# Three PSUM banks in a fixed order, a projection two chunks late and re-dealt weight splits in a fused linear-attention layer

## The chip, the cores and the metric

The kernel runs on one NeuronCore of a Trainium2 chip. The metric is the device time of one execution in microseconds (us); three executions of the kernel before took 1916.09, 1921.84 and 1921.94 us (median 1921.84).

## What is computed

x has 2048 rows (tokens) of 512 values. The layer is a gated linear attention with a small expert mixture ahead of it and behind it:

```python
x = x + 0.5 * ffn(layernorm(x))        # router of 64, top 8, mix of expert biases
x = x + attn(layernorm(x))
x = x + 0.5 * ffn(layernorm(x))

# attn: 32 query heads, 8 key/value heads, D = 128, chunks of 128 tokens
q, k, v = rope(x @ Wq.T), rope(x @ Wk.T), x @ Wv.T
dt = softplus(x @ Win.T + dt_bias);  g = dt * A;  G = cumsum(g) within a chunk
y_intra = (q @ k.T * decay) @ (v * dt)             # inside a chunk, causal
y_inter = (q * exp(G)) @ state                     # from the chunks before
state   = state * exp(G_last) + (k * exp(G_last - G)).T @ (v * dt)
y = (y_intra + y_inter) / rms * gnorm_w * silu(x @ Wg.T)
out = y @ Wo.T
```

## The kernel before

Every float32 operand of a large product is split into two bfloat16 halves, hi (a rounded copy) and lo (what is left), and each product is three matmuls, hi by hi, lo by hi and hi by lo (`mm3`, L288 to L290). So wherever a matrix is made, ScalarE (ACT) writes the hi half and VectorE (DVE) or GpSimd (POOL) subtracts for the lo half.

**The order of the work.** After a first mixture stage, the attention runs over 8 key/value heads g (called groups here), each with its 4 query heads. A group has 16 steps n, one for each chunk of 128 tokens, and s = n mod 4 is the step's place in a block of four. Each engine has a written-out order of its operations in its own `step` function, and semaphores alone tie the engines together; an engine never passes an operation that waits. Beside the attention of chunk n, the steps also compute the projections of the next block of 512 tokens, ten "fills" per block: item 0 is the key, items 1 to 4 the four query heads, item 5 the value and items 6 to 9 the gates of four chunks. `FILLS` says which item stands in slot A, B or C of which step.

On TensorE a step is: scores of chunk n+1, slot A, `read_state` (the state's part of the output), `turn_z` (transposes of the gated output z of chunk n-1), `attend` (the part inside the chunk, and the state update), slots B and C, in s=1 the key transposes, and `project_out` (z of chunk n-1 by Wo).

**PSUM.** The fills and the output projections share two banks in turn (`RING`, L150), numbered by `ring_order`. A writer waits until the use before the last of the ring is free (L692, L778). The fills of items 0 to 4 are read by ACT (`swap`, L867: two half copies into QS) and by DVE (`rotate`, L1220: product with cos into QF, L1233, which frees the bank; later the sum with the sine part, L1237, after POOL's `times_sin`, L1078). The value is read by ACT and DVE (`values`, `v_lo`), a gate by ACT (tanh into TH, L894) and DVE (`silu2`, L1253), and the output of a projection by DVE (`add_out`, L1333, into ACC). One further bank, B_T, takes the transposes of z and of the keys.

**The output of a chunk.** DVE multiplies the state's part by exp(G) (`combine`, L1276), adds it to the inner part (L1280); ACT squares it with a running sum (`square`, L936), POOL makes the inverse root (`inv_rms`, L1117 and L1120), DVE multiplies it with the gate (`gated`, L1313); after the transpose ACT and DVE split it (`zt_hi`, L943, `zt_lo`, L1329). The decay of the scores goes over POOL's `mask_rows` (L1091), ACT's `decay` (L907), DVE's `decayed` (L1267), ACT's `p_hi` (L913) and POOL's `p_lo` (L1113); the weighted value over POOL's `weighted_v` (L1101), ACT's `wv_hi` (L920) and POOL's `wv_lo` (L1109); the state over DVE's `update_state`, ACT's `state_hi` and DVE's `state_lo`.

**The weights.** A group needs 14 pieces of 128x512: 0 to 9 for the fills (four of them the gate's) and 10 to 13 for Wo. They are loaded into two staging buffers in turn (`STAGE`, `load_piece`, L325), so load i waits for the lo half of piece i-2. ACT writes the hi half (`split_hi`, L854; Wo is multiplied by half the norm's gain on the way), DVE or POOL the lo half (`w_lo` L1322, `wo_lo` L1317, `split_lo` L1070). Pieces 0 to 9 of the next group are split in steps 10 to 13 (`EARLY` on DVE, `MID` on POOL), the four Wo pieces all in step n=1 of the group itself, on ACT and DVE. The fills of the next group begin in step 12, and the projection with the new Wo in n=1.

**The loop.** Step 0 of the first group is written ahead, groups 0 to 6 are a loop of steps 1 to 16, and the last group is written out. A piece of code that ends the kernel is the second mixture stage.

Of the kernel before, what the change touches and what calls it, by code (L numbers as in the profile page):

```python
# [22 lines left out]
P = 128  # L23
# [3 lines left out]
G = H // KVH  # L27
# [15 lines left out]
FILLS = {0: {"A": 0, "B": 1, "C": 2}, 1: {"A": 3, "B": 4, "C": 5}, 2: {"A": 6, "B": 7}, 3: {"A": 8, "C": 9}}  # L43

EARLY = {10: (0, 1), 11: (3, 4), 12: (6,), 13: (8,)}
MID = {10: (2,), 11: (5,), 12: (7,), 13: (9,)}
LOADS = {1: (0, 1), 10: (2, 3, 4), 11: (5, 6, 7), 12: (8, 9), 13: (10, 11)}
N_EARLY = sum(len(i) for i in EARLY.values())
FIRST = len(FILLS[0])


def steps(last):

    return range(1, NCH if last else NCH + 1)
# [7 lines left out]
def ring_order(last):  # L62

    seq = []
    for n in steps(last):
        f = filled(n, last)
        seq += [("F", n // BLK, f[x]) for x in "ABC" if x in f] + [("W", n - 1)]
    if last:
        seq.append(("W", NCH - 1))
    order = {u: r for r, u in enumerate(seq)}  # L70
    order[("W", -1)] = -1
    return order


def turn_order(last):

    seq = []
    for n in steps(last):
        seq.append(("Z", n - 1))
        if n % BLK == 1 and filled(n, last):  # L80
            seq.append(("K", n // BLK))
    if last:
        seq.append(("Z", NCH - 1))
    return {u: r for r, u in enumerate(seq)}
# [12 lines left out]
def build(nc, x, cos, sin, masks, wall, rwt, rb, eb2, wint, dtb, alog, gn, out):  # L97
    rows_dram = nc.dram_tensor("rows_dram", (NCH, KVH, GW), F32).ap()
    with ExitStack() as ctx:
# [31 lines left out]
        NGT = sb("NGT", [P, NB, P])  # L131
# [18 lines left out]
        RING = BANK[0:2]  # L150
# [7 lines left out]
        with ExitStack() as over:  # L158
            MASKS, ONES, DTB, ALOG, SPD, GF = memory(over, (
                ("MASKS", [P, 3, P], F32), ("ONES", [P, P], F32), ("DTB", [P, H], F32), ("ALOG", [P, H], F32),  # L160
                ("SPD", [P, 2, 7, BLK * H], F32), ("GF", [P, NCH * H], F32)))
# [8 lines left out]
        SQ = sb("SQ", [P, G, P])  # L170
# [3 lines left out]
        ZTH = sb("ZTH", [P, GW], BF16)  # L174
        ZTL = sb("ZTL", [P, GW], BF16)
# [18 lines left out]
        QF = sb("QF", [P, 2, TB])  # L194
# [11 lines left out]
        TH = sb("TH", [P, GW])  # L206
# [1268 lines left out]
```

## Time and profile before

| | |
|---|---|
| three runs | 1916.09, 1921.84, 1921.94 us |
| the profiled execution | 1920.05 us, span 1918.3 us |
| mean granted TensorE clock | 0.967 |
| TensorE (PE) busy | 1712.5 us, 89% |
| weight loads (PEld) | 980.7 us, 51% |
| DVE | 1483.4 us, 77% |
| ACT | 1114.1 us, 58% |
| POOL | 1172.3 us, 61% |

All numbers come from one execution of the program, taken by the hardware profiler. Lines are those of the kernel's source. In a row of the timeline the first number is the start in us from the span's start, the second the duration; a bracket gives the engine's idle time before and the operation that ended it. Matmuls are pipelined: the next starts before the record of the one before ends. The clock column is the granted TensorE clock as a share of 2.4 GHz.

### The profile page before, as it was taken

How to read it: one execution, taken by the hardware profiler on the slowest of the kernel's cores; microseconds unless marked ns; L12 is line 12 of the kernel's file. 1: busy time of each engine (PE TensorE's matmuls, PEld its weight loads, DVE VectorE, ACT ScalarE, POOL GpSimd, SP SyncE). 2: the span in 40 equal slices, each digit the busy share in tenths (PEclk: the TensorE clock that was granted, in tenths of full speed). 3: DMA queues.
4: the chain of work that ended last, by engine and by line, in shares of the span. 5: the costliest groups of instructions: out<-in, count | busy, mean ns of one | idle time of the engine just before them, and what ended most of it. 6: DMA issues, size and time to landing. Idle time of an engine off the chain costs nothing.

```text
span 1918.3 us, 39511 instructions
## 1 busy us (share of the span) xinstructions
PE 1712.5 (89%) x11652; PEld 980.7 (51%) x11652; DVE 1483.4 (77%) x3212; ACT 1114.1 (58%) x3012; POOL 1172.3 (61%) x1084
## 2 busy tenths in 40 slices
PE   5657998989988998989988998999988998999976
PEld 5534554555545554555545554555545554555544
DVE  6976778787787778777787778778887778787875
ACT  5445556656665656656665565655665655665643
POOL 1236667656666667657665666656765766666643
PEclk8779999999999999999999999999999999999997
DMA  4110101110111001110111002110111002110002
GB/s 165 34 32 30 33 23 56 40 44 20 40 56 41 23 23 62 34 46 18 40 55 41 23 23 63 33 46 23 43 48 46 18 23 67 28 34 23 23 1 88
DMA packets 38532, 77.20 MB, mean 40 GB/s; under 512 B 4769, under 2 KB 5793, under 8 KB 37153
## 3 DMA queue, kind: packets, MB, share of 16 engines
q1 hardware_dynamic: 38304, 74.47, 12.6%
q8 instruction: 107, 1.75, 0.4%
q14 instruction: 121, 0.98, 0.2%
HBM read 69.99 MB, written 4.46 MB: 39 GB/s over the span
## 4 chain that ended last, share of the span: by engine, by line
PE 46%; issue 18%; DVE 15%; ACT 12%; POOL 7%; DVEq 1%; ACTq 1%; DMA 0%; POOLq 0%
PE B L288 14%; PE B L290 13%; PE B L289 13%; ACT SQ L936 3%; ACT QS L873 2%; DVE QF L1237 2%; PE B L774 2%; POOL ROWS L1091 2%; DVE QF L1233 1%; ACT QS L872 1%; PE B L455 1%; DVE PF L1267 1%; DVE YF L1276 1%; DVE ZTL L1329 1%; POOL WVF L1101 1%
## 5 line engine op out<-in xcount | busy, mean ns | idle before, releaser
L1113 POOL TENSOR_TENSOR PL<-PF,PH 128x512 bf16<-128x512 f32 x128 | 155.7, 1217 | 393.4 <-ACT PH L913 393.4
L288 PE MATMUL B<-WH,XTH 128*128 128x512 bf16 (+1 forms) x1024 | 295.2, 308 | 67.0 <-DVE QF L1233 57.0
L289 PE MATMUL B<-WL,XTH 128*128 128x512 bf16 (+1 forms) x1024 | 294.5, 307 | 0.0
L290 PE MATMUL B<-WH,XTL 128*128 128x512 bf16 (+1 forms) x1024 | 294.2, 307 | 0.0
L1078 POOL TENSOR_TENSOR QS<-QS,SIN 128x512 f32<-128x512 f32 x160 | 215.4, 1346 | 71.5 <-ACT QS L873 71.5
L288 PE MATMUL B<-XTH,WH 128*128 128x512 bf16 x640 | 242.7, 379 | 15.0 <-DVE G L1253 10.9
L290 PE MATMUL B<-XTH,WL 128*128 128x512 bf16 x640 | 242.6, 379 | 0.0
L289 PE MATMUL B<-XTL,WH 128*128 128x512 bf16 x640 | 242.6, 379 | 0.0
L288 PE MATMUL B<-WH,ZTH 128*128 128x512 bf16 x512 | 194.5, 380 | 36.9 <-DVE QF L1233 22.7
L913 ACT ACTIVATE PH<-PF 128x512 bf16<-128x512 f32 x128 | 80.7, 631 | 238.2 <-DVE PF L1267 238.1
L1329 DVE TENSOR_TENSOR ZTL<-B,ZTH 128x512 bf16<-128x512 f32 x128 | 88.1, 688 | 149.7 <-ACT ZTH L943 149.7
L290 PE MATMUL B<-WH,ZTL 128*128 128x512 bf16 x512 | 194.0, 379 | 0.0
L289 PE MATMUL B<-WL,ZTH 128*128 128x512 bf16 x512 | 194.0, 379 | 0.0
L1091 POOL TENSOR_TENSOR ROWS<-ROWS,AFTER 128x512 f32<-128x512 f32 x128 | 191.0, 1492 | 0.0
L936 ACT ACTIVATE SQ<-B 128x128 f32<-128x128 f32 x512 | 134.1, 276 | 84.8 <-DVE B L1280 83.4
L288 PEld LDWEIGHTS B<-WH,XTH 128*128 128x128 bf16 x1024 | 104.6, 102 | 149.5 <-DVE QF L1233 59.0
L907 ACT ACTIVATE PF<-ROWS,NG 128x128 f32<-128x128 f32 x512 | 162.6, 396 | 13.7 <-issue 13.7
L1267 DVE SCALAR_TENSOR_TENSOR PF<-B,DT,PF 128x128 f32<-128x128 f32 x512 | 143.8, 344 | 34.0 <-ACT PF L907 32.6
L920 ACT ACTIVATE WVH<-WVF 128x512 bf16<-128x512 f32 x120 | 75.6, 630 | 160.3 <-POOL WVF L1101 158.4
L1109 POOL TENSOR_TENSOR WVL<-WVF,WVH 128x512 bf16<-128x512 f32 x120 | 139.8, 1165 | 45.4 <-ACT WVH L920 45.4
L1313 DVE SCALAR_TENSOR_TENSOR YF<-B,RR,G 128x128 f32<-128x128 f32 x512 | 143.2, 341 | 7.3 <-POOL RR L1120 7.3
L1120 POOL TENSOR_TENSOR RR<-RM,HALF 128x4 f32<-128x4 f32 x128 | 137.1, 1071 | 19.0 <-POOL RM L1117 17.7
(160 smaller groups left out, 4539.9 us busy)
## 6 DMA issues: line engine op xcount, KB each, us to landing
ROWS<-rows_dram SPq DMA_DIRECT2D x128, 256.0 KB, 3.1
STAGE<-in_wall SPq DMA_DIRECT2D x112, 256.0 KB, 2.6
ACC<-in_x SPq DMA_DIRECT2D x4, 1024.0 KB, 7.6
out<-ACC SPq DMA_DIRECT2D x3, 1024.0 KB, 3.9
COS<-in_cos SPq DMA_DIRECT2D x1, 1024.0 KB, 12.6
SIN<-in_sin SPq DMA_DIRECT2D x1, 1024.0 KB, 14.4
out<-ACC SPq DMA_DIRECT2D x4, 256.0 KB, 2.5
EBF<-in_eb SPq DMA_DIRECT2D x1, 256.0 KB, 4.3
```

The costliest lines, as they stand in the source:

```text
L288: nc.tensor.matmul(out_, ah, bh, start=first, stop=False)
L289: nc.tensor.matmul(out_, ah, bl, start=False, stop=False)
L290: return nc.tensor.matmul(out_, al, bh, start=False, stop=last)
L907: ins = nc.scalar.activation(PF[:, c], ROWS[:, n % 2, c], ACT.Exp, bias=tab(NG, g, n)[:, h:h + 1], scale=-1.0)
L936: ins = nc.scalar.activation(SQ[:, h, :], B_PV[:, h * P:(h + 1) * P], ACT.Square, scale=float(P) ** -0.5, accum_out=SS[:, h:h + 1])
L1078: nc.gpsimd.tensor_tensor(QS[:, sl, :], QS[:, sl, :], SIN[:, t0:t0 + TB], ALU.mult).then_inc(sin_ready.sem, 1)
L1091: nc.gpsimd.tensor_tensor(rows, rows, AFTER[:, None, :].broadcast_to([P, G, P]), ALU.add).then_inc(rows_masked.sem, 1)
L1109: nc.gpsimd.tensor_tensor(WVL[:, :], WVF[:, :, :].rearrange("p h e -> p (h e)"), WVH[:, :], ALU.subtract).then_inc(wvl_ready.sem, 1)
L1113: nc.gpsimd.tensor_tensor(PL[:, n % 2, :], PF[:, :], PH[:, n % 2, :], ALU.subtract).then_inc(pl_ready.sem, 1)
L1120: nc.gpsimd.tensor_tensor(RR[:, :], RM[:, :], HALF[:, :], ALU.pow).then_inc(rr_ready.sem, 1)
L1267: ins = nc.vector.scalar_tensor_tensor(PF[:, c], B_S[:, c], dt[:, h:h + 1], PF[:, c], ALU.mult, ALU.mult)
L1313: ins = nc.vector.scalar_tensor_tensor(YF[:, c], B_PV[:, c], RR[:, h:h + 1], G2[:, s + b % 2 * (s == BLK - 1), c], ALU.mult, ALU.mult)
```

## The change

1. **Banks.** The ring has three banks (0, 1, 3). Which fill and which projection uses which one is written down (`FILL_BANK`, `OUT_BANK`, and `OUT_BANK_END` for the last steps), and so is whose release a writer waits for (`AFTER_FILL`, or the `add_out` of chunk n-3). Fills and outputs have semaphores of their own.
2. **Projection.** `project_out` in step n is that of chunk n-2; in s=1 it stands ahead of slot B, otherwise at the end. ZTH and ZTL have two buffers. The key transposes move from s=1 to s=2, `keys_lo` to s=3.
3. **Gain.** The norm's gain is applied when z is split (`zt_hi`, `zt_lo`), no longer to Wo.
4. **Splits.** All 14 pieces go by the same code. `HI`, `LO_POOL`, `LO_DVE` and `LOADS` deal them over steps 9 to 13 and, for Wo, steps 17 and 18 (n = 1 and 2 of the next group). ACT copies at the end of its step (in s=1 ahead of slot C, in s=2 ahead of the keys), POOL subtracts after wv_lo, DVE after `gated` and ahead of slot B.
5. **Scaling.** ACT multiplies the state's part by exp(G), four 128x128 pieces into YF (`scale_inter`), between `zt_hi` and `wv_hi`; DVE's product is gone.
6. **Orders.** ACT computes the decay of chunk n+2 late in step n rather than that of n+1 at its start; POOL masks rows after `weighted_v`; item 4's lo half moves from DVE to the end of POOL's step s=2; QF has four buffers; item 9 moves to slot B.
7. **Memory.** The squares go into YF, the tanh into its slot of G2, NGT shares memory with the set-up tensors.
8. **The loop** covers steps 3 to 18; steps 0 to 2 are written ahead (`PEEL`).

```diff
+PEEL = 3
+FILLS = {0: {"A": 0, "B": 1, "C": 2}, 1: {"A": 3, "B": 4, "C": 5}, 2: {"A": 6, "B": 7}, 3: {"A": 8, "B": 9}}
+FILL_BANK = (0, 1, 2, 1, 0, 1, 2, 0, 2, 1)
+OUT_BANK = (0, 2, 1, 2)
+OUT_BANK_END = {10: 1, 11: 2, 12: 0, 13: 1, 14: 0, 15: 1}
+AFTER_FILL = {0: 3, 1: 2, 3: 2, 5: 2, 7: 3, 8: 2}
...
-EARLY = {10: (0, 1), 11: (3, 4), 12: (6,), 13: (8,)}
-MID = {10: (2,), 11: (5,), 12: (7,), 13: (9,)}
-LOADS = {1: (0, 1), 10: (2, 3, 4), 11: (5, 6, 7), 12: (8, 9), 13: (10, 11)}
+HI = {9: (0,), 10: (1, 2), 11: (3, 4, 5), 12: (6, 7, 8), 13: (9,), 17: (10, 11), 18: (12, 13)}
+LO_POOL = {9: (0,), 10: (1,), 11: (3, 5), 12: (6, 7), 13: (9,), 17: (10,), 18: (12,)}
+LO_DVE = {10: (2,), 11: (4,), 12: (8,), 17: (11,), 18: (13,)}
+LOADS = {3: (0, 1), 9: (2,), 10: (3, 4), 11: (5, 6, 7), 12: (8, 9), 13: (10, 11), 18: (12, 13)}
...
-        RING = BANK[0:2]
+        RING = (BANK[0], BANK[1], BANK[3])
...
+            def bank_free(g, n, item, use):
...
+                elif item in AFTER_FILL:
+                    pe.wait_ge(ring_free.sem, ring_free.at(g, use - AFTER_FILL[item]))
+                else:
+                    pe.wait_ge(out_free.sem, out_free.at(g, n - 3))
...
+            def scale_inter(g, n):
...
+                act.wait_ge(inter_full.sem, inter_full.at(g, in_event(n)))
+                eg = tab(EG, g, n)
+                for h in range(G):
+                    c = slice(h * P, (h + 1) * P)
+                    ins = nc.scalar.activation(YF[:, c], B_IN[:, c], ACT.Copy, scale=eg[:, h:h + 1])
+                ins.then_inc(inter_read.sem, 1)
...
-                nc.scalar.activation(ZTH[:, :], B_T[:, :], ACT.Copy).then_inc(zth_ready.sem, 1)
+                nc.scalar.activation(ZTH[:, n % 2, :], B_T[:, :], ACT.Copy, scale=GNH[:, 0:1]).then_inc(zth_ready.sem, 1)
...
-                nc.vector.tensor_tensor(YF[:, :].rearrange("p (h e) -> p h e", h=G), B_IN[:, :].rearrange("p (h e) -> p h e", h=G),
-                                            tab(EG, g, n)[:, :, None].broadcast_to([P, G, P]), ALU.mult).then_inc(inter_read.sem, 1)
```

The new order of a step on DVE, in full (`now` is the step's fills; TensorE, ACT and POOL have new orders of the same kind):

```python
if nxt: decayed(g, n + 1)
if s == 1 and now: add(FILLS[0]["C"])
if s == 2 and now: v_lo(g, b + 1, use(PV_)); add(FILLS[1]["B"])
if s != 2 and n >= PEEL: add_out(g, n - 3, last)
if s == 1 and now: q_lo(g, b + 1, FILLS[0]["B"])
if s == 3 and now: keys_lo(g, b + 1)
if now: slot("A")
combine(g, n); update_state(g, n)
if n: zt_lo(g, n - 1)
if s < 2 and now: add(now["A"])
state_lo(g, n)
gated(g, n)
if s == 1 and n >= PEEL: add_out(g, n - 2, last)
if s == 1 and now: q_lo(g, b + 1, FILLS[0]["C"])
for i in weights_at(LO_DVE, n, last): w_lo(g + 1 if n >= PEEL else g, i)
if now: slot("B")
if s == 0 and now: add(now["B"]); slot("C")
```

ACT: `p_hi`(n+1), hi of the item before (s=1), slot A, hi (s=2), `zt_hi`(n-1), `scale_inter`, hi (s=1), `wv_hi`(n+1), `square`, `state_hi`, slot B (s other than 1), hi of A (s=0), `decay`(n+2), slot C (s=0), slot B and hi of A (s=1), the hi halves of `HI`, slot C (s=1), `keys_hi` (s=2). POOL: `p_lo`(n+1), `weighted_v`(n+1), lo of A's item of the step before (s=1, 2), sine A, `mask_rows`(n+2), `inv_rms`, sine B (s=0), `wv_lo`(n+1), lo of item 4 (s=2), sine B (s=1), the lo halves of `LO_POOL`, sine C (s=0).

## Rows read from the trace of the kernel before

**Rows 1.** The page, busy time and share of each engine, instructions.

```profile
PE 1712.5 (89%) x11652; PEld 980.7 (51%) x11652; DVE 1483.4 (77%) x3212; ACT 1114.1 (58%) x3012; POOL 1172.3 (61%) x1084
```

**Rows 2.** The line L1289: count, duration min/median/max (ns), first and last start (us).

```profile
L1289 DVE COPY ST<-B x8: 681/681/681, 167.4 to 1669.2; 128x512 f32<-128x512 f32 x8
```

**Rows 3.** Timeline of TensorE, the first matmul of four steps: start, us, operation.

```profile
622.01 0.38 PE L288 MATMUL B<-QH,KH 128*128 128x512 bf16 x1
...
632.86 0.38 PE L288 MATMUL B<-QH,KH 128*128 128x512 bf16 x1
...
643.95 0.38 PE L288 MATMUL B<-QH,KH 128*128 128x512 bf16 x1
...
657.38 0.38 PE L288 MATMUL B<-QH,KH 128*128 128x512 bf16 x1
```

**Rows 4.** Timeline of TensorE, a V fill and the transposes behind it.

```profile
666.57 0.23 PE L288 MATMUL B<-WH,XTH 128*128 128x128 bf16 x1 [0.77 <-DVE QF L1233]
...
669.26 0.28 PE L721 MATMUL B<-IDF,KF 128*128 128x128 f32 x1
```

**Rows 5.** Waits of TensorE in one group, 596.5 to 811: us in total, times, longest.

```profile
PE B L288 <- DVE QF L1233: 10.7, 8, 4.5
PE B L288 <- DVE G L1253: 3.8, 3, 1.5
PE B L288 <- issue: 1.0, 1, 1.0
```

**Rows 6.** Timeline of TensorE, the longest wait of that group, in step n=1.

```profile
614.66 0.23 PE L288 MATMUL B<-WH,XTH 128*128 128x128 bf16 x1 [4.47 <-DVE QF L1233]
```

**Rows 7.** Two stretches: us, busy us (and instructions) per engine, PEclk, DMA share, GB/s.

```profile
616.00:618.00 2.00, 2.00 (x22) 2.00 (x21) 2.00 (x7) 1.94 (x10) 1.43 (x3) 0.50 0.02 4
...
1686.50:1689.00 2.50, 2.40 (x23) 2.40 (x24) 2.47 (x8) 1.27 (x10) 2.31 (x2) 0.51 0.29 90
```

**Rows 8.** Timeline of ACT: half a swap, then four squares, ended by the state copy.

```profile
653.01 0.59 ACT L873 ACTIVATE QS<-B 64x512 f32<-64x512 f32 x1
653.62 0.28 ACT L936 ACTIVATE SQ<-B 128x128 f32<-128x128 f32 x1
...
654.63 0.64 ACT L927 ACTIVATE STH<-ST 128x512 bf16<-128x512 f32 x1
```

**Rows 9.** Groups by line and shape: busy us, mean ns | idle us before, releaser.

```profile
L1120 POOL TENSOR_TENSOR RR<-RM,HALF 128x4 f32<-128x4 f32 x128 | 137.1, 1071 | 19.0 <-POOL RM L1117 17.7
...
L1109 POOL TENSOR_TENSOR WVL<-WVF,WVH 128x512 bf16<-128x512 f32 x120 | 139.8, 1165 | 45.4 <-ACT WVH L920 45.4
...
L1233 DVE TENSOR_TENSOR QF<-B,COS 128x512 f32<-128x512 f32 x128 | 87.5, 684 | 38.8 <-ACT QS L873 37.9
...
L1276 DVE TENSOR_TENSOR YF<-B,EG 128x512 f32<-128x512 f32 x120 | 81.7, 681 | 0.3 <-PE B L774 0.3
...
L1324 DVE TENSOR_TENSOR WL<-STAGE,WH 128x512 bf16<-128x512 f32 x42 | 58.4, 1417 | 23.1 <-ACT WH L857 23.1
...
L857 ACT ACTIVATE WH<-STAGE 128x512 bf16<-128x512 f32 x80 | 48.1, 621 | 10.2 <-DMA STAGE<-in_wall 10.2
...
L1072 POOL TENSOR_TENSOR WL<-STAGE,WH 128x512 bf16<-128x512 f32 x38 | 44.9, 1185 | 34.1 <-ACT WH L857 34.1
...
L860 ACT ACTIVATE WH<-STAGE,GNH 128x512 bf16<-128x512 f32 x32 | 21.1, 708 | 0.0
```

**Rows 10.** The load of a weight piece, L331, all 112.

```profile
DMA to landing us min/median/max: 2.3/2.6/14.3
```

**Rows 11.** Timeline of TensorE, two further waits: start of the fills, last group.

```profile
128.16 0.39 PE L288 MATMUL B<-XTH,WH 128*128 128x512 bf16 x1 [3.27 <-DVE KF L1233]
...
1686.60 0.29 PE L288 MATMUL B<-WH,XTH 128*128 128x128 bf16 x1 [3.20 <-DVE QF L1233]
```

**Rows 12.** Timeline of TensorE, transposes of z in two of the last four steps.

```profile
1826.19 0.63 PE L774 MATMUL B<-IDF,YF 128*128 128x128 f32 x4 [0.44 <-DVE YF L1313]
...
1834.25 0.63 PE L774 MATMUL B<-IDF,YF 128*128 128x128 f32 x4 [0.44 <-DVE YF L1313]
```

More of the change, by code:

```diff
@@ L75, in turn_order, with use_of, z_turn, k_turn @@
[L75 to L84, printed above, removed]
+def use_of(b, item):
+    return NFILL * b + item
+def z_turn(n, last=False):
+    return n + 1 + min((max(n - 1, 0) + BLK - 1) // BLK, NB - 1 if last else 2 * NB)
+def k_turn(b):
+    return (BLK + 1) * (b - 1) + 3 if b else 0
@@ L87, in cs_event, with fill_bank, out_bank @@
+def fill_bank(use):
+    b, item = divmod(use, NFILL)
+    return FILL_BANK[item] if b else (item + 2) % 3
+def out_bank(n, last):
+    return OUT_BANK_END[n] if last and n in OUT_BANK_END else OUT_BANK[(n + 2) % BLK]
 def cs_event(n):
@@ L353, in _ @@
             load_rows(0, 2)
-            load_rows(0, 3)
             def step(g, n, last):
@@ new lines, in step, with slot @@
+                now = filled(n, last)
+                back = filled(n - 1, last) if n else {}
+                nxt = not (last and n == NCH - 1)
+                def slot(x):
+                    item = now[x]
+                    if item < PV_:
+                        swap(g, b + 1, item, use_of(b + 1, item))
+                    elif item == PV_:
+                        values(g, b + 1, use_of(b + 1, item))
+                    else:
+                        gate(g, b + 1, item - PG, use_of(b + 1, item))
@@ new lines, in step, with use, slot, add @@
+                now = filled(n, last)
+                nxt = not (last and n == NCH - 1)
+                def use(item):
+                    return use_of(b + 1, item)
+                def slot(x):
+                    if now[x] < PV_:
+                        times_cos(g, b + 1, now[x], use(now[x]))
+                    else:
+                        silu2(g, b + 1, now[x] - PG, use(now[x]))
+                def add(item):
+                    add_sin(g, b + 1, item, use(item))
+                if nxt:
+                    decayed(g, n + 1)
@@ new lines, in step @@
+                if s == 1 and now:
+                    add(FILLS[0]["C"])
+                if s == 2 and now:
+                    v_lo(g, b + 1, use(PV_))
+                    add(FILLS[1]["B"])
+                if s != 2 and n >= PEEL:
+                    add_out(g, n - 3, last)
+                if s == 1 and now:
+                    q_lo(g, b + 1, FILLS[0]["B"])
+                if s == 3 and now:
+                    keys_lo(g, b + 1)
+                if now:
+                    slot("A")
@@ L1388, in step @@
+                combine(g, n)
                 update_state(g, n)
-                slot("A", 1)
-                if filled(n, last).get("B", PG) < PG:
-                    slot("B", 0)
+                if n:
+                    zt_lo(g, n - 1)
+                if s < 2 and now:
+                    add(now["A"])
                 state_lo(g, n)
```

490 lines of the change are left out of this document (224 added, 266 removed).

## The prediction

> **What bounds the kernel now.** I read the page's shares first, then the state's copy (it marks the groups), TensorE's timeline for steps without a wait, and TensorE's own waits in one group. TensorE is busy 89% of the span and no other engine over 77% [rows 1]. The span has three parts: a start up to 167.4 us, eight rounds over key/value heads (I call one a group, 16 steps n, kind s = n mod 4), and a tail. The state's copy at n = 0 runs eight times, 167.4 to 1669.2, so a group lasts (1669.2 - 167.4)/7 = 214.55 us [rows 2].
>
> What would TensorE need without waits? Undisturbed steps show it: s=2 takes 632.86 - 622.01 = 10.85 us (s=3 has the same work), s=0 takes 657.38 - 643.95 = 13.43 [rows 3]. Step s=1 differs from s=0 by the V fill, 669.26 - 666.57 = 2.69 in place of 2.59 (12 issues of 0.216) [rows 4], and has the 0.44 of the key transposes: 13.97. Four steps are 49.1, four blocks 196.4, less the state read missing at n=0 (0.67) and the state update at n=15 (0.65): **195.1 us**. So 19.45 us of each group are lost. TensorE's waits there sum to 15.5: 10.7 in eight waits ended by a rotation (QF L1233), 3.8 in three ended by a gate (G L1253), 1.0 at the loop's edge [rows 5]. Some 2.0 more is pipeline tail (12 waits by 0.38 - 0.22, the part of a matmul's record past the next issue, not counted as idle). The rest is clock: after the 4.47 us wait of n=1, behind the Wo splits [rows 6], the granted clock is 0.50, the lower level of 1.2 GHz, and the fill takes 4.3 in place of 2.69, so 1.6 lost [rows 7]. Nearly all of it is waiting for one of two PSUM banks.
>
> **The three banks.** A bank's next writer now comes two TensorE pieces after its last, at least 2.6 + 2.6 + 0.65 = 5.85 us. Its readers need two half copies (0.6 each) and a product (0.68), 2.0 with hand-offs, behind other work [rows 8, 9]. By a walk through the queues with those durations every bank of an ordinary block is free in time: the nearest case, the bank of item 6, is freed by the extra add of step s=1 at about 12.6 and wanted at 14.2. So the 15.5 + 2.0 + 1.6 go, apart from the loop's edge (1.0 and its tail, **1.2**), which stays. That alone is -18.2 per group. Projecting two chunks late makes ZTH and ZTL no longer urgent; it costs no TensorE time, since the matmuls are the same.
>
> **The scaling.** DVE loses L1276, 0.68 x 120, and ACT gains four 128x128 pieces per step. Nearest row: the four squares of a step, from the same kind of bank and with their accumulator reads, run from 653.62 to 654.63, so 1.0 [rows 8]. The ends are 0.8 (without the reads) and 1.3 (a longer start for the scale operand); I take 1.05. It is idle ACT time, but it lies in a chain: z's transpose of n-1 (4.5 after the step's start), ZTH 0.6, scaling 1.05, combine 0.7, squares 1.0, RM and RR on POOL 1.4, all with hand-offs, 9.6; then WVL 1.17 [rows 9] and only then, in s=2, the low half of item 4 (1.2): 11.95. The next step's scores need that half at 11.29. Likewise the key transposes, at 8.25 in s=2, need ZTL(n-1), which now stands behind combine and the state update and ends at 8.7. The two overlap: **0.75** per block, three blocks, 2.3; by ends 0 to 1.2 each. The Trainium skill (ScalarE: Activation LUTs, "What ACT_TABLE_LOAD costs") says that each [128,1] pointer operand adds about 93 ns. The weight copies bear it out, 707 with the gain and 615 without [rows 9]. By it ZTH too is 0.09 longer, the stall 0.85, and nothing else moves.
>
> **What costs nothing.** ACT's exponentials a step earlier have their rows masked by then; the tanh into G2 in place waits for a z of four steps back; NGT in shared memory adds one wait, once, for row sends long landed; squares into YF come after combine has read it; add_out moved by two chunks fills DVE's wait for p. POOL's masking moved behind p_lo and WVF is part of the walk above. Without that cover each would cost DVE or ACT its own 0.6 to 1.2 per step, far below their idle time.
>
> **The weight splits.** All 14 pieces share two staging buffers: load i waits for the low half of i-2, and takes 2.6 us to land [rows 10]. Write hi(i) for ACT's bf16 copy and lo(i) for the low half of piece i. DVE does 5 splits per group instead of 10 (-7 us), POOL 9 instead of 4 (+5.8, at 1.16) [rows 9]; neither is the bound. What matters is where they stand. Times are from the step's first matmul.
> - Step 12. DVE's low half of piece 8 stands **before** the products of items 1 and 2. Piece 8 can't be loaded before POOL's low half of piece 6, and ACT copies piece 6 only after the swap of item 2. At the earliest: item 2 full 11.05, swap 12.25, hi(6) 12.85, lo(6) 14.0, issue and landing 16.8, hi(8) 17.4, lo(8) on DVE 18.8, product of item 1 19.5. Item 3, first fill of step 13, wants that bank at 13.43 + 0.65 = 14.08: at least 5.4 us of wait. But step 11 already ends with ACT held: lo(3) is done at 12.25, load 5 lands at 15.0, hi(5) ends at 15.6, which is 4.75 into step 12 with everything queued behind it (p_hi, swap, ZTH, scaling, squares, STH, swap, hi, exponentials), so the swap of item 2 ends at 14.8, 2.6 late. I take **8.05**, the longer, since no queue on the way has an empty place. SP's rows load waits behind these loads too, but is needed two steps on.
> - Clock. After 4.47 us idle the level fell and 1.6 was lost, so I take **1.6**; up to 3.4 if the slow stretch covers more than one fill. A gap of 3.20 was followed by 0.51 too [rows 7, 11]. [...]
> - Step 13 to 14. POOL is late by the same chain; lo(9) ends at 15.55 and item 6, which needs it, is wanted at 14.2: **1.35** (0 to 2.5). Step 10 adds **0.1** by the late keys_lo.
> - Steps 17, 18 (n = 1, 2 of the next group). The Wo pieces 12 and 13 are copied at the end of step 18, but the projection in that same step reads them. lo(11) on DVE delays step 18's start by 1.7, the key transposes by 1.4, hi(12) ends at 11.4, lo(12) behind item 4's half at 14.45. TensorE wants it at 11.4: 1.4 + 3.1 = **4.5** (3.0 to 5.5) and for the 3.1 gap half a clock loss, **0.8** (0 to 1.6).
>
> **Sum.** 195.1 + 1.2 + 2.3 + 8.05 + 1.6 + 1.35 + 0.1 + 4.5 + 0.8 = 215.0 per group, against 214.55: +0.45, seven times, +3.2. Last group: no next weights. Before, 3.2 + 0.16 + 1.6 (its Wo) and two block ends of 1.5, 8.0; after, 4.5 + 0.8 + 1.5 = 6.8: -1.2. Start: TensorE's 3.27 wait for the first product [rows 11] goes, -3.3. Last four steps have no fills and run from transpose to transpose in 1834.25 - 1826.19 = 8.06 [rows 12]; my chain after is 8.3 with the later gated product and p_hi ahead of ZTH, so 0. Final mixture stage: the same code, 0. The profiled execution took 1920.05 us (span 1918.3); 1920.05 + 3.2 - 1.2 - 3.3 = 1918.75, said as **1919**. That execution lies 0.1% under the median 1921.84, so no correction.
>
> **Rivals.**
> 1. *Side queues recover* (chance 0.36, faster): the step 12 wait is its lower end 5.4, the Wo wait 3.0 without clock loss, lo(9) and the small waits hardly reach TensorE. 195.1 + 1.2 + 5.4 + 1.6 + 3.0 + 1.0 = 207.3, 7 x -7.25 = -51, with start and last group (-6): 1863. For it: ACT and POOL are idle over a third of a group. Against: they idle inside a chain that is serial. If the wait didn't reach TensorE at all, 199 per group and about 1805; chance 0.03 inside this case.
> 2. *The chain through the staging buffers is longer* (0.27, slower): in step 12, one more us in ACT's or POOL's queue, 9.5; clock 3.4; lo(9) 2.5; Wo 5.5 + 1.6; blocks 3.3: 222.1, 7 x 7.55 = +53, 1969; halfway 1942. It decides from 215.5 per group on. For it: the wait runs through four engines and two transfers, and any of them can only add.
> 3. *The change doesn't do what it says*: TensorE waited for something other than banks, the stalls stay and the new ones add. The rotation product that frees the banks is named as what ended ten of the waits' microseconds [rows 5], so 0.03; 214.5 + 15 x 7, over 2000.
> 4. Forecast, stalls of banks traded for waits on splits, within 1% either way: 0.34.
>
> **Numbers.** Chances by a measurement's bound of 0.3% (1914 to 1926): the forecast case gives 0.19 inside it, 0.07 faster, 0.08 slower; with the rivals faster 0.43, same 0.19, slower 0.38. The range takes rival 1 down to 1862 and rival 2 up to 1962. The forecast's own range is 1900 to 1938.
>
> **What would show it.** Right: per group some 215 between copies of ST at n=0; no TensorE wait on a rotation or gate in n = 3 to 9; one wait of 7 to 9 us ahead of a fill between steps 12 and 13, DVE's WL split idle just before it for as long, and low clock after; a wait of about 3 in the middle of the projection after n=2, for a split; ACT about 64% busy, DVE about 70%. Wrong: the wait of step 13 under 6 (rival 1) or over 9 (rival 2), or waits on banks in ordinary blocks (rival 3).

## The result, and the profile of the kernel after

The median is 1941.54 us (1936.86 to 1945.57, four runs) against 1921.82 for the kernel before: a ratio of 1.0109, with a 95% interval of 1.0077 to 1.0142. The change makes the kernel slower by 1.1%. The profiled execution took 1938.87 us, its span is 1937.1. As ahead of the prediction I read the page first, then the copy of the state, which marks the groups.

The page's busy times, then the line of the state's copy (count, ns min/median/max, first and last start in us); they answer to [rows 1, 2]:

```profile
PE 1721.9 (89%) x11652; PEld 973.2 (50%) x11652; DVE 1327.3 (69%) x3023; ACT 1247.2 (64%) x3492; POOL 1224.7 (63%) x1153
...
L1324 DVE COPY ST<-B x8: 678/680/681, 162.6 to 1687.6; 128x512 f32<-128x512 f32 x8
```

TensorE has the same 11652 instructions, and VectorE's load went from 77% to 69%: work was moved as meant. A group now lasts (1687.6 - 162.6)/7 = 217.86 us, where it was 214.55. Seven times 3.31 is +23.2; the start is 4.8 shorter (162.6 against 167.4), and what follows the last copy, the last group and the tail, is 0.4 longer. The sum is the 18.8 by which the spans differ.

TensorE's waits over the whole run (us in total, times, longest), the largest of those inside the groups:

```profile
PE B L298 <- DVE QF L1273: 57.2, 8, 7.9
PE B L298 <- POOL WL L1105: 26.7, 15, 2.9
PE B L728 <- DVE ZTL L1359: 23.3, 31, 2.0
...
PE B L298 <- issue: 18.4, 7, 3.5
```

The waits for banks of [rows 5], some eleven per group on rotations and gates, are gone. In their place stand a few long ones, once a group each. One group's timeline of TensorE, 598.3 to 816.2, the rows with a wait over 0.1 us (start, duration, operation, wait and releaser):

```profile
626.11 0.65 PE L728 MATMUL B<-IDF,KF 128*128 128x128 f32 x4 [1.49 <-DVE ZTL L1359]
...
630.79 0.60 PE L298 MATMUL B<-WH,ZTH 128*128 128x512 bf16 x1 [2.73 <-POOL WL L1105]
...
636.12 0.39 PE L298 MATMUL B<-QH,KH 128*128 128x512 bf16 x1 [2.61 <-issue]
...
682.88 0.65 PE L728 MATMUL B<-IDF,KF 128*128 128x128 f32 x4 [0.49 <-DVE ZTL L1359]
...
768.99 0.60 PE L298 MATMUL B<-XTH,WH 128*128 128x512 bf16 x1 [7.68 <-DVE QF L1273]
...
785.91 0.39 PE L298 MATMUL B<-WH,XTH 128*128 128x512 bf16 x1 [0.66 <-POOL WL L1105]
```

The row with 0.49 comes twice more, at 732.91 and 794.18. In order: key transposes and projection of step 18 (the Wo pieces), the loop's edge, an ordinary block, the first fill of step 13, item 6. All eight sum to 16.64 us. The 7.68 has the chain that the prediction walked through. ScalarE and VectorE ahead of it:

```profile
751.37 0.63 ACT L875 ACTIVATE WH<-STAGE 128x512 bf16<-128x512 f32 x1 [3.69 <-DMA STAGE<-in_wall]
...
766.81 0.63 ACT L875 ACTIVATE WH<-STAGE 128x512 bf16<-128x512 f32 x1 [3.38 <-DMA STAGE<-in_wall]
```

```profile
767.48 0.69 DVE L1354 TENSOR_TENSOR WL<-STAGE,WH 128x512 bf16<-128x512 f32 x1 [6.16 <-ACT WH L875]
768.09 0.68 DVE L1273 TENSOR_TENSOR QF<-B,COS 128x512 f32<-128x512 f32 x1
```

ScalarE is held twice for a load, VectorE stands 6.16 us in front of the low half of piece 8, and the product that frees the bank (L1273) is next in its queue. The clock, by stretches (us; busy and instructions of PE, PEld, DVE, ACT, POOL; PEclk, DMA share, GB/s):

```profile
632.00:634.00 2.00, 1.52 (x4) 0.30 (x2) 0.00 (x0) 0.00 (x0) 0.00 (x0) 0.50 0.84 251
...
644.00:760.00 116.00, 114.90 (x783) 63.59 (x782) 84.60 (x189) 83.97 (x242) 83.21 (x77) 1.00 0.11 35
...
768.00:770.00 2.00, 1.01 (x3) 0.43 (x4) 1.97 (x4) 0.00 (x0) 0.00 (x0) 0.50 0.52 182
770.00:772.00 2.00, 2.00 (x7) 0.65 (x5) 2.00 (x7) 0.76 (x2) 0.05 (x1) 0.50 0.13 46
772.00:774.00 2.00, 2.00 (x6) 0.71 (x5) 1.55 (x2) 0.39 (x1) 2.00 (x2) 0.50 0.00 0
```

From 644 to 760 TensorE is busy for 114.9 of 116 us at full clock: this is what the three banks gave. After the 7.68 the clock is 0.50 (the level of 1.2 GHz) for the whole next fill.

The loop has seven passes and so six taken branches. TensorE's wait on issue at them, six times in this run, is 2.46 to 3.46 us, 2.93 on average (the shown group has 2.61); in the kernel before the same six are 0.72 to 1.03, 0.89 on average. The seventh wait in the line above, 0.86 us, lies at 159.10, ahead of the loop.

### The profile page after: what moved, and what is told of

Its sections match the earlier page's. It is cut to its first block, busy times and chain, and to the rows that moved or that the text cites. A ratio compares the mean times of both kernels' runs of the same rounds, so it can differ in the third digit from the quotient of the medians.

```text
span 1937.1 us, 39986 instructions
## 1 busy us (share of the span) xinstructions
PE 1721.9 (89%) x11652; PEld 973.2 (50%) x11652; DVE 1327.3 (69%) x3023; ACT 1247.2 (64%) x3492; POOL 1224.7 (63%) x1153
## 4 chain that ended last, share of the span: by engine, by line
PE 48%; POOL 21%; issue 14%; ACT 7%; DVE 7%; DMA 2%; ACTq 0%; DVEq 0%; POOLq 0%; SPq 0%
PE B L298 15%; PE B L299 14%; PE B L300 14%; POOL QS L1111 4%; POOL WVL L1142 3%; POOL WL L1105 3%; POOL RR L1153 2%; ACT YF L958 2%; POOL ROWS L1124 2%; POOL WVF L1134 2%; DMA STAGE<-in_wall 2%; PE B L781 1%; ACT YF L968 1%; DVE ST L1329 1%; POOL RM L1150 1%
## 5 line engine op out<-in xcount | busy, mean ns | idle before, releaser
L298 PE MATMUL B<-WH,XTH 128*128 128x512 bf16 (+1 forms) x1024 | 286.7, 304 | 4.7 <-POOL WL L1105 4.7
L299 PE MATMUL B<-WL,XTH 128*128 128x512 bf16 (+1 forms) x1024 | 286.3, 304 | 0.0
L300 PE MATMUL B<-WH,XTL 128*128 128x512 bf16 (+1 forms) x1024 | 285.6, 303 | 0.0
L299 PE MATMUL B<-XTL,WH 128*128 128x512 bf16 x640 | 249.2, 389 | 0.0
L1315 DVE TENSOR_TENSOR B<-B,YF 128x512 f32<-128x512 f32 x120 | 83.9, 699 | 165.1 <-ACT YF L958 165.1
L1153 POOL TENSOR_TENSOR RR<-RM,HALF 128x4 f32<-128x4 f32 x128 | 154.8, 1210 | 19.0 <-POOL RM L1150 17.7
L1124 POOL TENSOR_TENSOR ROWS<-ROWS,AFTER 128x512 f32<-128x512 f32 x128 | 162.5, 1270 | 0.0
L968 ACT ACTIVATE YF<-B 128x128 f32<-128x128 f32 x512 | 135.3, 285 | 33.0 <-DVE B L1315 33.0
L1105 POOL TENSOR_TENSOR WL<-STAGE,WH 128x512 bf16<-128x512 f32 x75 | 100.8, 1349 | 63.2 <-ACT WH L875 63.2
L1134 POOL TENSOR_TENSOR WVF<-VF,WJ 128x512 f32<-128x512 f32 x120 | 138.8, 1156 | 0.0
```

The costliest lines, as they stand in the source:

```text
L298: nc.tensor.matmul(out_, ah, bh, start=first, stop=False)
L299: nc.tensor.matmul(out_, ah, bl, start=False, stop=False)
L300: return nc.tensor.matmul(out_, al, bh, start=False, stop=last)
L968: ins = nc.scalar.activation(YF[:, h * P:(h + 1) * P], B_PV[:, h * P:(h + 1) * P], ACT.Square, scale=float(P) ** -0.5, accum_out=SS[:, h:h ...
L1105: nc.gpsimd.tensor_tensor(WL[:, i, :], STAGE[:, i % 2, :], WH[:, i, :], ALU.subtract).then_inc(wl_of(i)[0].sem, 1)
L1124: nc.gpsimd.tensor_tensor(rows, rows, AFTER[:, None, :].broadcast_to([P, G, P]), ALU.add).then_inc(rows_masked.sem, 1)
```

## The experiments

What was open: whether one wait or the whole chain of splits carries the loss, what the loop's edge is, and whether a version without these waits beats both kernels. "Group" is the mean time between the eight copies of ST, "issue" a wait for which the profile names no releaser. Ratios are to the kernel before, run beside each, with a 95% interval; its median was 1919.66 to 1921.83. "After" stands for 1941.54 us and 217.86.

**1. The low half of piece 8 behind the slots** (VectorE's step).

```diff
+                if s:
                     for i in weights_at(LO_DVE, n, last):
                         w_lo(g + 1 if n >= PEEL else g, i)
...
                     slot("C")
+                if s == 0:
+                    for i in weights_at(LO_DVE, n, last):
+                        w_lo(g + 1 if n >= PEEL else g, i)
```

> Edit: in steps with s=0 DVE's low half of a weight piece (only piece 8, step 12) stands behind slots B and C, not ahead of them; nothing else. Order theory: TensorE's wait at the first fill of step 13 is DVE's product of item 1 standing behind that low half. The wait of 7.7 us, its 0.16 of tail and the 2.5 us that the fill behind it loses by the low clock go: -10.3 us in each of seven groups, -72; part of it comes back where item 6 waits for ScalarE and GpSimd, which piece 8 still holds (up to 3 us per group). 1870 to 1892 us against 1941. Rival, lateness of ScalarE and GpSimd themselves: the wait moves to another fill or to attend inside steps 13 and 14 at nearly its full size, 1930 or more.

Measured: 1943.54 us, 1.0106 [1.0069, 1.0142], group 217.76. Timeline of TensorE in steps 13 and 14:

```profile
766.95 0.39 PE L298 MATMUL B<-XTH,WH 128*128 128x512 bf16 x1 [1.22 <-DVE QF L1273]
...
787.19 0.61 PE L298 MATMUL B<-WH,XTH 128*128 128x512 bf16 x1 [5.49 <-POOL WL L1105]
```

The 7.68 fell to 1.22, and item 6's wait for piece 9 grew from 0.66 to 5.49, as the rival had it. So the place in VectorE's queue decides where most of the wait shows, and moving one split doesn't make the loads, copies and splits behind it any earlier. The rest of what was won went at the loop's edge: its six waits are 3.57 on average against 2.93, in this group 4.31 with a slow stretch behind it. Why the edge grew, no run took apart.

**2. The Wo pieces split in the middle of step 18.** ScalarE's part is shown; in the same way GpSimd's split stands behind mask_rows and VectorE's behind zt_lo where n % NCH is 2.

```diff
                 scale_inter(g, n)
+                if n % NCH == 2:
+                    next_weights()
...
-                next_weights()
+                if n % NCH != 2:
+                    next_weights()
```

> Edit: in step 18 (n=2) the splits of Wo pieces 12 and 13 stand in the middle of the step on each engine (ScalarE behind the scaling, GpSimd behind the masking, VectorE behind ZTL) and not at its end. Order theory: the 2.73 us wait inside the projection and its 0.16 go, and the low clock behind it (about 2 us by the sum). The 2.61 us at the loop's edge: if it is long because TensorE's queue was held by that wait just ahead of the branch, it falls to the 1.0 of the kernel before, in all -6.9 per group, 1893 us. If it is long because the weight loads issued at that moment slow the fetch of the loop's code, it stays and the gain is 5.0 to 5.3 per group: 1905 us. Rival: the projection needs those pieces no earlier than something else that ends at the same time, then nothing changes, 1941.

Measured: 1919.71, 0.9998 [0.9987, 1.001], group 214.86. So these two pieces' place cost 3.0 us per group, 1.1% of the kernel. TensorE at the edge and in the step behind it:

```profile
626.97 0.39 PE L298 MATMUL B<-QH,KH 128*128 128x512 bf16 x1 [1.93 <-POOL QL L1119]
...
633.23 0.93 PE L781 MATMUL B<-IDF,YF 128*128 128x128 f32 x4 [2.14 <-DVE KDL L1305]
```

The 2.73 is gone, and the profile names a releaser at the edge now, but two waits of 4.07 together have come, and a slow stretch behind them. The gain is three fifths of what was expected at least (5.0).

**3. The next head's first two loads two steps later.**

```diff
-LOADS = {3: (0, 1), ...
+LOADS = {5: (0, 1), ...
```

> Edit: pieces 0 and 1 of the next group are loaded in step 5 rather than in step 3, the first step of the loop's body. Fetch theory: at the loop's edge the two loads of 256 KB run at the same time as the fetch of the loop's code; without them TensorE's wait there falls from 2.61 to about 1.0 us, -1.6 per group, -11, 1930 us. Queue theory (the branch comes late since the Wo wait held TensorE's queue): nothing changes, 1941.

Measured: 1943.02, 1.0125 [1.0102, 1.0148], group 217.73. TensorE's wait on issue, whole run, and one edge:

```profile
PE B L298 <- issue: 13.2, 7, 2.2
```

```profile
636.41 0.60 PE L298 MATMUL B<-QH,KH 128*128 128x512 bf16 x1 [2.05 <-issue]
```

The six edges are 2.06 on average where they were 2.93, so loads in flight are 0.87 of it; in the shown group a stretch at the low clock behind the edge, which cost 1.9 us where the kernel after had none, took that back. Neither theory had that.

**4. TensorE kept busy through the gap of step 13.** This kernel repeats the scores product of one step eleven times, 33 products more per group with the same result.

```diff
+                for _ in range(11 if n == 14 and not isinstance(g, int) else 0):
+                    mm3(B_S[:, :], KH[:, par, t:t + P], KL[:, par, t:t + P], QH[:, par, :, t:t + P], QL[:, par, :, t:t + P],
+                        True, True)
```

> Edit: in the loop, step 13 issues its scores product twelve times instead of once (the same result, 33 more matmuls of 0.216 us = 7.1 us), so that TensorE works through the time in which it waited for the bank. Clock theory: the wait falls from 7.7 to about 0.5 us, the granted clock stays at full level, and the fill behind it takes 2.6 instead of 5.1 us: the group is 2.5 us shorter although more work is done, 7 x -2.5 = -17, 1924 us. Rival: the slow fill is something else than the clock's answer to the gap (its operands' or the bank's): the fill stays at 5.1 and the time at 1941; if VectorE's next product of scores waits for the repeats, it is slower, up to 1955.

Measured: 1933.77, 1.0091 [1.0058, 1.0125], group 217.10.

```profile
767.09 0.39 PE L298 MATMUL B<-XTH,WH 128*128 128x512 bf16 x1 [0.33 <-DVE QF L1276]
...
782.24 0.39 PE L298 MATMUL B<-WH,XTH 128*128 128x512 bf16 x1 [1.45 <-POOL WL L1108]
```

```profile
760.00:774.00 14.00, 13.67 (x84) 6.98 (x83) 7.17 (x13) 6.78 (x15) 8.01 (x8) 1.00 0.27 76
```

The clock stays at 1.00 and the fill takes 2.6 us again. That shows the clock's share by itself, but only 0.8 of the 2.5 us reach the group's time: the next wait, which depends on the other engines, grew by 0.8, and the group had a slow stretch behind its edge that cost 1.7. (1924 us was expected.)

**5. ZTL ahead of combine and state update.**

```diff
+                if n:
+                    zt_lo(g, n - 1)
                 combine(g, n)
                 update_state(g, n)
```

> Edit: on VectorE the low half of z stands ahead of combine and the state update, not behind them; nothing else. Order theory: TensorE's waits ahead of the key transposes (three of 0.49 us and one of 1.49 per group) go, and with their tails the group is at most 3.5 us shorter; in step 18 the Wo wait behind takes its 1.5 back (it ends by the clock of GpSimd), so 1.5 to 2.0 per group, 1927 to 1931 against 1941.5. Rival, the clock pays it: waits elsewhere grow by as much, 1941.

Measured: 1941.83, 1.0121 [1.0103, 1.0138], group 218.21.

```profile
PE B L298 <- POOL WL L1105: 42.3, 15, 5.4
...
PE B L298 <- POOL QL L1116: 10.7, 14, 0.8
```

The ZTL waits went. In blocks the low half of item 4 (QL) took their place with 0.76, and the Wo wait grew by what the key transposes no longer waited: the rival's 1941. The prediction had put both limits at nearly the same price.

**6. Two pieces per step, one low half per engine**, loads a step earlier, ScalarE's copies right behind state_hi.

```diff
+HI = {9: (0, 1), 10: (2, 3), 11: (4, 5), 12: (6, 7), 13: (8, 9), 17: (10, 11), 18: (12, 13)}
+LO_POOL = {9: (0,), 10: (2,), 11: (4,), 12: (6,), 13: (9,), 17: (10,), 18: (12,)}
+LO_DVE = {9: (1,), 10: (3,), 11: (5,), 12: (7,), 13: (8,), 17: (11,), 18: (13,)}
...
                 state_hi(g, n)
+                next_weights()
```

> Edit: the pieces are dealt two per step (steps 9 to 13, 17, 18), one low half on GpSimd and one on VectorE, each loaded one step before it is needed, and ScalarE copies them right behind the state's high half instead of at the end of its step; nothing else. Staging theory: no engine waits any more for a load that waits for a split of the same step; the waits of step 13 (7.7) and of item 6 (0.7) and the clock loss behind them (about 2.5) go: -10 to -11 per group, about 1868 us. The Wo wait and the edge stay as they are or shrink by up to 1.5 with ScalarE's earlier copies. Rival, seen when only VectorE's order was changed (the wait moved on to item 6): what limits steps 12 to 14 is the sum of split work and not its place; then a wait of over 5 us turns up at item 6 again and the time is 1930 or more.

Measured: 1910.34, 0.9948 [0.9932, 0.9965], group 213.86.

```profile
616.21 0.65 PE L728 MATMUL B<-IDF,KF 128*128 128x128 f32 x4 [1.62 <-DVE ZTL L1359]
...
626.26 0.60 PE L298 MATMUL B<-QH,KH 128*128 128x512 bf16 x1 [3.56 <-issue]
...
772.00 0.43 PE L298 MATMUL B<-WH,XTH 128*128 128x512 bf16 x1 [2.46 <-DVE WL L1354]
```

The 7.68 is a 2.46 at item 6 now, so most of it came of this deal: three pieces in each of steps 11 and 12, with ScalarE's copies at the end of the step. The run changed deal, loads and the copies' place together and doesn't say which did how much. The group is 4.0 us shorter and not 10 to 11, since what went there came in part elsewhere: item 6 waits 1.8 longer than in the kernel after, with 1.7 of low clock behind it, one block's key transposes 1.1 longer, and the edge is 3.56 with a slow stretch behind it that cost 3.2.

**7. All of it together**: 6, with 2, 3 and 5, and item 4's low half on VectorE.

> Edit: the even deal, z's low half first, the Wo pieces of step 18 in the middle of the step, item 4's low half on VectorE behind slot A, pieces 0 and 1 loaded in step 5. By the sum of the prediction nothing is left but the loop's edge: 195.1 + 1.2 to 3 per group, with a remainder of 1 to 3 us of small waits in steps 2 and 3: 198 to 201, so 1941.5 - 7 x 17 to 20 and some 5 in the last group: 1797 to 1818 us. That beats both kernels. Rival: the loop's edge grows (its wait has grown to 4.3 us where other waits went), and with it a slow stretch: 204 to 206 per group, 1845 us.

Measured: 1846.89 (1840.54 to 1851.22), 0.9623 [0.9592, 0.9655], group 204.56. Faster than both kernels, but outside the 1797 to 1818 expected: it is the rival's 1845 with a group of 204 to 206. TensorE's waits, whole run:

```profile
PE B L298 <- issue: 18.4, 7, 3.2
PE B L298 <- DVE WL L1358: 17.3, 7, 2.5
PE B L298 <- POOL WL L1108: 11.2, 8, 1.4
```

**8. The scaling back on VectorE.**

```diff
-                scale_inter(g, n)
...
+                nc.vector.tensor_tensor(YF[:, :].rearrange("p (h e) -> p h e", h=G), B_IN[:, :].rearrange("p (h e) -> p h e", h=G),
+                                            tab(EG, g, n)[:, :, None].broadcast_to([P, G, P]), ALU.mult).then_inc(inter_read.sem, 1)
```

> Edit: the state's part is scaled by VectorE again, as in the kernel before, instead of by ScalarE; all else as in the changed kernel. Chain theory: the chain from z's transpose to the combine loses 0.6 (ZTH) and 1.05 (four pieces) and gains 0.7, about 1 us less per step; ZTL ends 1 us earlier or at the same time, so TensorE's waits of 0.49 ahead of the key transposes go and the waits on splits shrink by up to 1 us each: -2 to -4 per group, 1915 to 1928. Rival, ScalarE's relief for VectorE is worth its chain: VectorE's longer queue (0.7 us per step) delays its low halves, no change or slower, 1941 to 1950.

Measured: 1930.86, 1.0067 [1.0045, 1.0088], group 216.64, 10.7 us less than after (whose interval, from 1.0077, overlaps this one a little), and 3 us above the range expected.

```profile
PE B L298 <- POOL WL L1104: 36.8, 15, 4.4
...
PE B L728 <- DVE ZTL L1362: 5.4, 8, 1.3
```

Moving the scaling to ScalarE lengthened the chain and costs here, some 1.2 us per group: the ZTL waits fall from 23.3 to 5.4 in the whole run, of which the Wo wait takes 10.1.

**9. The edge without a wait of TensorE ahead of it**: run 7 with GpSimd's order changed.

```diff
+                if n % NCH == 2:
+                    for i in weights_at(LO_POOL, n, last):
+                        split_lo(g + 1 if n >= PEEL else g, i)
                 if not (last and n >= NCH - 2):
                     mask_rows(g, n + 2)
```

> The kernel of e7_all_fixed with one edit: in step 18 GpSimd splits the low half of piece 12 (Wo) ahead of mask_rows instead of behind it, 1.26 us earlier, so that TensorE's wait of 1.42 us for it just ahead of the loop's branch goes to 0.2 us or less. Theory Q (TensorE's own queue stands in that wait, so it comes to the branch late and the first instructions of the next pass are fetched only then): the edge's issue wait falls from 3.14 us to about 1.0 to 1.5 us, and the group becomes 1.3 us for the Wo wait + 1.6 to 2.1 us for the edge + up to 1 us of clock shorter: 204.6 to about 201, time 1819 to 1830 us. Rival F (the fetch is slow by itself, by what the DMA queues carry or by what the other engines fetch at the same time): the edge stays at 2.6 to 3.2 us and the group falls by 1.3 us alone, to 203.3; time 1835 to 1840 us. Rival D (what is late is the data of the first step behind the branch): the wait at the edge is put down to a half of ScalarE, VectorE or GpSimd instead of issue.

Measured: 1835.95, 0.9566 [0.9546, 0.9586], group 204.01. TensorE at the edge, and VectorE's split of piece 13:

```profile
602.90 0.60 PE L298 MATMUL B<-QH,KH 128*128 128x512 bf16 x1 [3.32 <-issue]
```

```profile
597.30 1.22 DVE L1358 TENSOR_TENSOR WL<-STAGE,WH 128x512 bf16<-128x512 f32 x1
```

The Wo wait is gone and the edge is 3.32, not 1.0 to 1.5. So theory Q fell as it was put, and the time is the one of rival F. But the last piece ends at 598.52, and the first of its products starts at 598.77 without idle time: the wait costs TensorE nothing and yet is released late.

**10. Item 6 waits piece by piece**, and in step 13 VectorE's w_lo stands right behind state_lo.

```diff
                     for k in range(KT):
+                        if fresh and item == PG:
+                            pe.wait_ge(wh_ready.sem, wh_ready.at(gw, PG + k))
+                            signal, i = wl_of(PG + k)
+                            pe.wait_ge(signal.sem, signal.at(gw, i))
```

> The kernel of e9_edge_no_wo_wait, and the last wait of step 13 taken up: item 6 (the first gate fill of a new head) waits for each of its four weight pieces just ahead of that piece's products instead of for all four at its start, and VectorE splits piece 8 right behind state_lo (it stood idle 0.9 us there) instead of behind the low half of q. Theory (the 2.48 us of item 6 are a wait for data that are there 2 us before the last product wants them): the wait at item 6 goes to 0.3 us or less, nothing else of that size takes its place since piece 9 is wanted 1.95 us into the fill, and the group is 2.2 to 2.5 us shorter than that of e9: 17 us less over seven groups, some 1 us of clock with each at most. Rival (lateness of ScalarE and VectorE is only moved, as in e1_w8_last): a wait of 1 to 2 us appears at the scores of step 14 or at item 7, and the gain is under 7 us.

Measured: 1818.43 (1816.14 to 1820.58), 0.947 [0.9454, 0.9486], group 200.94, 17.5 us less than run 9, where 17 was expected.

```profile
597.77 0.39 PE L298 MATMUL B<-QH,KH 128*128 128x512 bf16 x1 [3.38 <-issue]
```

Of item 6's wait 0.26 is left; one of 3.38 at the edge is the largest of the group.

**11 and 12. What holds the edge.** Run 11 is run 10 with the Wo pieces 1 us earlier and all four waited for ahead of the first product. Run 12 is the kernel before with two waits, long released, ahead of the last three products of a group.

```diff
-                    if n % NCH == 0:
-                        pe.wait_ge(wh_ready.sem, wh_ready.at(g, n // NCH * NPIECE + PO + h))
...
+                    if n % NCH == 0 and h == 0:
+                        for i in range(PO, PO + G):
+                            pe.wait_ge(wh_ready.sem, wh_ready.at(g, n // NCH * NPIECE + i))
+                            signal, k = wl_of(i)
+                            pe.wait_ge(signal.sem, signal.at(g, n // NCH * signal.per + k))
```

```diff
+                    if n % NCH == NCH - 1 and h == G - 1:
+                        pe.wait_ge(zth_ready.sem, zth_ready.at(g, n))
+                        pe.wait_ge(turn_free.sem, turn_free.at(g, turn_use))
```

> The kernel of e10_gate_halves with project_out(16), the last work ahead of the loop's branch in step 18, waiting for all of its four Wo pieces ahead of its first product instead of for each piece ahead of its own three products; so that they are there, step 18 splits pieces 12 and 13 first on each engine (ScalarE ahead of zt_hi, VectorE behind zt_lo, GpSimd behind weighted_v), 1 us earlier. Theory Q2 (TensorE's queue passes a wait only once the products ahead of it are issued, even where it is long released; the first instructions of the next pass are fetched when the queue has passed its last wait, and the first product of the pass runs some 3.8 to 4.2 us behind that; so in the kernel before, with 12 products of 0.216 us behind the last wait, 1.03 us of it show, and here, with 3 products, 3.4): with 12 products behind the last wait the edge's issue wait falls from 3.38 us to 1.0 to 1.6 us, 7.5 us of issue in seven groups instead of 21, and the group from 200.9 to about 198 to 199 us; time 1800 to 1808 us. Rival F (the fetch is slow by itself in this kernel, whatever stands in TensorE's queue): the edge stays at 3.0 us or more and the time within 4 us of 1818. A wait of up to 0.8 us for WL at the start of project_out may come in both.

> The kernel before with two waits added and nothing else: in the project_out that is the last work ahead of the loop's branch, TensorE waits again for zth_ready and turn_free, with the values that it has waited for 9 products earlier (both long reached), ahead of the last three products. Theory Q2 (a wait that is released already still keeps the queue from reaching the branch early): the edge's issue wait rises from 1.03 us to 2.8 to 3.4 us, and with the clock that it costs the group by 2 to 3 us: 1934 to 1942 us, the size of what the change lost. Rival R (only a wait that is really late holds the queue): edge 1.0 us, time within 0.3% of 1920. Rival F (fetch slowed by other traffic or by the other engines' fetches): the same as R.

Measured, run 11: 1817.87 (1816.51 to 1818.8), 0.9459 [0.9443, 0.9475], group 200.69; TensorE, and VectorE's last Wo split:

```profile
596.52 0.39 PE L298 MATMUL B<-QH,KH 128*128 128x512 bf16 x1 [1.23 <-issue]
...
602.83 0.65 PE L787 MATMUL B<-IDF,YF 128*128 128x128 f32 x4 [2.23 <-DVE KDL L1309]
```

```profile
591.24 1.16 DVE L1365 TENSOR_TENSOR WL<-STAGE,WH 128x512 bf16<-128x512 f32 x1
```

Run 12: 1921.3, 0.9995 [0.9985, 1.0004]; TensorE at the edge:

```profile
603.66 0.39 PE L288 MATMUL B<-QH,KH 128*128 128x512 bf16 x1 [0.97 <-issue]
```

Run 12 says that a wait already released costs nothing (rival R), so Q2 in its strong form fell too. Run 11 says that the edge shrinks, from 3.35 to 1.36 on average over the six, when the last release is early against the last product; rival F, with 3.0 or more, fell. What remains is a reading that fits all runs, though none shows TensorE's queue itself: the queue runs ahead of the products, a wait that is still closed holds it, and the next pass starts a nearly fixed time after that release, whether 3 products follow it (runs 9 and 10) or 12 (run 11). The shown edges agree: from the end of the last Wo split to the first product behind the branch pass 602.90 - 598.52 = 4.38 us in run 9, 4.44 in run 10 (split ended 593.33) and 596.52 - 592.40 = 4.12 in run 11. After, where GpSimd's split was the last, it is 636.12 - 630.73 = 5.39, and 636.41 - 632.22 = 4.19 with the loads moved (run 3), so the load traffic is the other 1.2. GpSimd after and in run 3:

```profile
629.13 1.60 POOL L1105 TENSOR_TENSOR WL<-STAGE,WH 128x512 bf16<-128x512 f32 x1
```

```profile
630.62 1.60 POOL L1105 TENSOR_TENSOR WL<-STAGE,WH 128x512 bf16<-128x512 f32 x1
```

Run 11's 2.15 us at the edge came back in the next step as a 2.23 on KDL: the other engines were no earlier. So the last fix gave nothing where 10 to 18 us were expected, and runs 10 and 11 stand equal as the fastest, 5.3% and 5.4% under the kernel before.

## Why the prediction was wrong

It forecast no change (1919 us), with 0.43 for faster and 0.38 for slower; the time came out slower, 1.1% by an interval clear of 1, inside the range of 1862 to 1962. The profiled execution is 20.1 us over the sum: 7 x (217.86 - 215.0) = 20.0, the last group 1.6 more, the start 1.5 less. By terms of the shown group, with 0.16 of pipeline tail for each wait:

- **The bank waits go**: right. No rotation or gate holds a fill in the ordinary steps. And the 195.1 that TensorE needs without waits holds: summed with the undisturbed distances between products, the group after has 195.2.
- **Step 12 to 13, 8.05**: measured 7.68 + 0.16 = 7.84. The place, the releaser and VectorE's idle time were as put. Rival 1, that the side queues recover, didn't come.
- **Wo, 4.5**: 1.49 + 2.73 + 0.32 = 4.54. **Item 6, 1.35**: 0.82. **Three blocks, 2.3**: 3 x 0.65 = 1.95. **keys_lo, 0.1**: none seen. Together 0.9 under the sum.
- **The scaling, 1.05 per step**: measured 1.14 for the four pieces in a run's timeline. The Trainium skill (ScalarE: Activation LUTs, "What ACT_TABLE_LOAD costs") has about 93 ns for each [128,1] pointer operand; the copy of z's transpose with the gain has a mean of 686 ns, the plain copy of V from a bank 591, which agrees.
- **The loop's edge, 1.2: this step failed.** "Which stays" was taken from the one value before. Measured 2.61 + 0.16 = 2.77 here, and 2.93 without tail on average. The projection put ahead of the branch now waits for pieces that the other engines have just split, and two loads fly at the same time (251 GB/s in the stretch above). The first product behind the branch comes 5.39 us after the last split, and with the loads moved 4.19 (run 3). The prediction costed the wait of the Wo pieces, and not what their late release does to the branch behind it: +1.6.
- **The clock, 1.6 + 0.8: this step failed.** The remainder is 217.86 - 195.1 - 16.64 - 8 x 0.16 = 4.84. Of it the fill behind the 7.68 lost 2.5 (768.99 to 774.08 instead of 2.59), the six products behind the Wo wait 1.3 (0.43 apart instead of 0.216). Of the last 1.0 some 0.45 is no clock but two holds under 0.1 us with their tails, ahead of the scores at 686.19 and 736.22, and 0.3 is that this group took 217.56 and the mean is 217.86; the rest stays open. The estimate took its 1.6 from a fill behind a wait of 4.47 [rows 6, 7], which was slow for a part only: of 614.66 to 618.98 its products ran at half rate up to 618.10. Behind 7.68 the whole fill was slow. Both are inside the ends that the prediction gave (3.4 and 1.6), and the two terms together are short by 1.4, the remainder by 2.4.

1.6 + 2.4 - 0.9 - 0.2 are the 2.9 by which the group was missed, within rounding. It lies above the 215.5 from which rival 2 was to decide, but not by the mechanism in its name: the chain through the staging buffers was no longer than forecast. Only its dearer clock came true in part.

Three smaller slips don't change the forecast. The -18.2 of the banks is 19.45 less the edge's 1.2, while the terms named with it, 15.5 + 2.0 + 1.6, add up to 19.1 and leave -17.9. The edge is counted seven times, and the loop branches back six times. And 707 and 615 ns are the medians of the weight copies, where [rows 9] print the means, 708 and 621.

**Start, -3.3**: measured -4.8. **Last group, -1.2**: +0.4 with the tail. No run took either apart.

## What to carry to other kernels

Freeing the bottleneck of its many small waits gives nothing while a longer serial chain (here load, high half, low half, over two buffers and four engines) ends in it once per pass; deal such work evenly, one per step and engine, before judging the gain: the same change with an even deal and a few places in the queues put right is 5.3% faster than the kernel before (run 10) instead of 1.1% slower. A wait ahead of a loop's branch may have to be released well ahead of it, not merely in time for its own product: in run 9 such a wait cost no idle time of its own, and the first product behind the branch still came 4.38 us after it. And a removed wait is worth what the next one leaves of it: runs 1, 5 and 11 each took one away and gained nothing.

## What was not expected of the hardware

- **The loop's edge follows the last release.** Over the six taken branches of each run, the first product of a pass came 4.0 to 4.7 us after the last split had ended (runs 2, 3, 7, 9, 10, 11), and 5.0 to 5.9 where two weight loads were in flight (after, runs 1, 4, 5, 6, 8). Run 2 has these loads too and lies at 4.0 to 4.4, but there the packet named below starts at 624.05, before they are issued at 624.73. With no late release the wait at the edge is 0.7 to 1.0 (the kernel before), and waits released long before add nothing (run 12). The Trainium skill (Advanced Engine Details and Errata, "Control Flow Timing") gives a branch about 51 ns, a compare and branch about 108. No edge here comes near that. What costs would be getting the next pass's first instructions, which was not measured apart from the branch. The traces point there: at all 84 taken branches of the 14 profiled kernels a 16 KB packet of the instruction queue q8 starts 2.6 to 3.3 us ahead of the pass's first product (in the kernel before at 598.79 for 601.76, in run 10 at 594.62 for 597.77). It starts 1.1 to 1.9 us after the last split, and 2.1 to 3.1 after it where the two loads are in flight, so the loads delay the start of this packet and not what comes behind it. That q8 carries TensorE's instructions is a reading of this regularity, not shown.
- **What a gap costs in clock can't be read from its length alone.** The 7.68 cost its whole fill, 2.5 us; filled with products (run 4) it cost none. In the kernel after, the gap of 2.73 at 630.79 has six products at half rate behind it and the next one, of 2.61 at 636.12, none. With the edge at 1.23 (run 11) each stretch of 2 us from 592 to 608 has a clock of 1.00, where behind the edge of 3.38 (run 10) 598 to 600 and 600 to 602 have 0.53 and 0.61.
